# One PSUM bank for the values, two for the first layer, and all orders made anew, in a macaron block on one core

## The reference, cut to what matters

```
def kernel_func(q, k):
    scores = einsum('bhqd,bhkd->bhqk', q, k) / sqrt(8)
    w = relu(scores)
    return w / (sum(w, axis=-1, keepdims=True) + 1e-6)
def attn(x):
    qkv = (x @ w_qkv).reshape(B, S, 16, 24)          # q, k, v of 8 each
    out = einsum('bhqk,bhkd->bhqd', kernel_func(q, k), v)
    y = x + out.reshape(B, S, 128) @ w_out + b_out
    return layernorm(y) * gamma + beta
def ffn(x):                                          # w1: 128 x 512, w2: 512 x 128
    h = layernorm(x) * ln_gamma + ln_beta
    return x + 0.5 * (silu(h @ w1 + fc1_bias) @ w2 + fc2_bias)
x = x + 0.5 * ffn(layernorm(x))
x = x + attn(layernorm(x))
x = x + 0.5 * ffn(layernorm(x))
```

## Time and profile before

| | us |
|---|---|
| median of three runs | 380.73 (380.62 to 382.76) |
| the profiled execution | 380.02 |
| its span, first to last instruction | 378.2 |
| TensorE busy | 368.9 (98%) |
| VectorE busy | 286.9 (76%) |
| ScalarE busy | 227.5 (60%) |
| GpSimd busy | 222.8 (59%) |
| mean granted clock of TensorE | 0.995 of 2.4 GHz |

### The profile page before, as it was taken

One profiled execution on the slowest core, in us unless ns is written; L12 is line 12 of the kernel. 1 busy time (PEld: TensorE's weight loads), 2 busy tenths in 40 slices (PEclk: granted clock), 3 DMA queues, 4 the chain that ended last, 5 costly groups with the idle time before them and its releaser, 6 DMA issues.

```text
span 378.2 us, 11748 instructions
## 1 busy us (share of the span) xinstructions
PE 368.9 (98%) x4590; PEld 191.0 (51%) x4590; DVE 286.9 (76%) x690; ACT 227.5 (60%) x421; POOL 222.8 (59%) x454
## 2 busy tenths in 40 slices
PE   8979999999999999999999999999999999999996
PEld 7863523453554445553564445553464444523596
DVE  4744788987868978788777978789777877887681
ACT  2446466666857476566857577466766577466504
POOL 7683065737972589438981589437991567146053
PEclk9998999999999999999999999999999999999999
DMA  5156004600361005400271005410170004500001
GB/s 167 29 99 154 4 0 95 158 3 2 72 154 58 3 1 145 120 20 0 57 172 58 0 2 119 124 41 0 39 185 34 2 2 113 140 3 1 2 3 59
DMA packets 14391, 23.05 MB, mean 61 GB/s; under 512 B 2688, under 2 KB 3968, under 8 KB 14336
## 3 DMA queue, kind: packets, MB, share of 16 engines
q1 hardware_dynamic: 11520, 17.83, 19.5%
q10 hardware_dynamic: 2816, 4.46, 3.8%
HBM read 3.41 MB, written 2.10 MB: 15 GB/s over the span
## 4 chain that ended last, share of the span: by engine, by line
PE 89%; DVE 5%; issue 2%; POOL 2%; ACT 1%; DMA 1%; ACTq 0%; POOLq 0%; DVEq 0%
PE o_bank L461 31%; PE scores L446 16%; PE pre_bank L404 10%; PE post_bank L404 9%; PE pre_bank L409 5%; PE pre_bank L410 3%; PE post_bank L409 2%; PE pre_bank L397 2%; PE pre_bank L423 2%; PE post_bank L423 2%; PE post_bank L410 2%; PE o_bank L391 1%; DVE probs L990 1%; PE post_bank L397 1%; PE pre_bank L477 1%
## 5 line engine op out<-in xcount | busy, mean ns | idle before, releaser
L990 DVE TENSOR_SCALAR probs<-scores 128x512 f32<-128x512 f32 x256 | 164.0, 682 | 49.1 <-PE scores L446 46.9
L719 ACT ACTIVATE probs<-scores 128x512 f32<-128x512 f32 x256 | 138.6, 596 | 67.0 <-PE scores L446 67.0
L461 PE MATMUL o_bank<-probs,v_op 128*32 128x512 f32 x1024 | 136.4, 605 | 0.0
L446 PE MATMUL scores<-q_op,k_op 32*128 32x512 f32 x512 | 78.1, 494 | 2.0 <-DMA q_op<-q_parts 1.5
L446 PEld LDWEIGHTS scores<-q_op,k_op 32*128 32x128 f32 x512 | 32.0, 181 | 85.8 <-issue 50.7
L619 ACT ACTIVATE pre_y<-pre_bank,b_sum,col_consts 128x512 f32<-128x512 f32 x28 | 21.8, 779 | 26.4 <-PE pre_bank L423 26.3
L461 PEld LDWEIGHTS o_bank<-probs,v_op 128*32 128x32 f32 x1024 | 21.6, 108 | 30.3 <-issue 25.9
L404 PE MATMUL pre_bank<-w,pre_y 128*32 128x128 f32 x960 | 30.8, 274 | 0.0
L1019 POOL TENSOR_SCALAR norm_x_var<-norm_x_mv 128x4 f32<-128x4 f32 x21 | 4.1, 196 | 44.3 <-DVE norm_x_mv L791 43.8
L404 PEld LDWEIGHTS pre_bank<-w,pre_y 128*32 128x32 f32 x960 | 25.5, 110 | 7.9 <-issue 7.4
L404 PE MATMUL post_bank<-w,post_y 128*32 128x128 f32 x960 | 29.3, 273 | 0.0
(11 more groups left out here) (185 smaller groups left out, 548.6 us busy)
## 6 DMA issues: line engine op xcount, KB each, us to landing
k_op<-k_parts SPq DMA_DIRECT2D x64, 128.0 KB, 2.6
q_op<-q_parts SPq DMA_DIRECT2D x63, 128.0 KB, 2.7
pre_x<-in_L_attn_x_dram ACTq DMA_DIRECT2D x7, 256.0 KB, 2.7
out_dram<-o_rows ACTq DMA_DIRECT2D x7, 256.0 KB, 2.1
w_int<-in_L_ffn_fc_q_dram SPq DMA_DIRECT2D x2, 256.0 KB, 4.0
rows<-in_lines_dram ACTq DMA_DIRECT2D x1, 256.0 KB, 6.3
s_rows<-in_L_ffn_fc_scales_dram SPq DMA_DIRECT2D x1, 256.0 KB, 6.0
out_dram<-o_rows ACTq DMA_DIRECT2D x2, 128.0 KB, 2.3
```

Of the source, the lines that this page charges most:

```text
L446: mm(scores[i][:, j, :], k_op[rows, g, P * kt:P * (kt + 1)], q_op[rows, g, :], start=True, stop=True).then_inc(scores_done[i], 1)
L461: last = mm(o_bank[pair][VW * j:VW * (j + 1), :], v_op[:, kt, heads_of(g).start + 2 * j, :], probs[:, s % 2, j, :], start=(odd == 0 and kt ...
L719: activation(probs[:, s % 2, j, :], scores[0][:, j, :], ACT.Relu).then_inc(probs_done[0], 1)
L990: v.tensor_scalar(probs[:, s % 2, 2 + j, :], scores[1][:, j, :], 0.0, None, ALU.max).then_inc(probs_done[1], 1)
```

## The change

The second `o_bank` is given up and its bank given to `pre`, whose fills now take two banks in turn; the ten fills of a batch are an even number, so each kind of fill always has the same bank (`hT`, `fc1.1`, `fc1.3`, `uT`, `q` the first; `fc1.0`, `fc1.2`, `fc2`, `k`, `v` the second). Each bank has its own semaphore of reads, and a fill waits for the fill two before it. `fc1` waits for `hT` to be read ahead of its first product, since the bank no longer says so. The values of a new pair wait for the transpose of the pair before, where they waited for the one before that. All order tables are new. The number of matmuls does not change. The core of the diff, with one or two lines of the tables:

```diff
-    ([], ["post.fc2.0@-2", "pre.fc1.0@1"]),
-    (["post.fc2.1@-2", "post.fc2.2@-2", "post.fc2.3@-2", "pre.fc1.1@1"], []),
...
+    ([], ["post.fc2.0@-2"]),
+    (["post.fc2.1@-2"], ["post.fc2.2@-2", "post.fc2.3@-2", "pre.hT@1"]),
...
+            def place(self, b, fill):
+
+                i = len(self.fills) * b + self.fills.index(fill)
+                return i % len(self.banks), i // len(self.banks)
...
+            def freed(self, b, fill):
+
+                return self.free(b, fill), self.place(b, fill)[1] + 1
...
-        pre, post = Stage("pre", PRE_FILLS), Stage("post", POST_FILLS)
+        pre, post = Stage("pre", PRE_FILLS, 2), Stage("post", POST_FILLS, 1)
...
-        o_bank = [psum(f"o_bank{i}", [P, S]) for i in range(2)]
+        o_bank = psum("o_bank", [P, S])
...
-                if free_before(st, b, fill) > 0:
-                    pe.wait_ge(st.free, free_before(st, b, fill))
...
+                i, before = st.place(b, fill)
+                if before > 0:
+                    pe.wait_ge(st.frees[i], before)
...
                     next_fill(st, b, what)
+                    pe.wait_ge(*st.freed(b, "hT"))
...
-                    if not odd and NP * b + pair - 1 > 0:
-                        pe.wait_ge(o_read, NP * b + pair - 1)
+                    if not odd and NP * b + pair > 0:
+                        pe.wait_ge(o_read, NP * b + pair)
...
-                        last = by_tokens((pre.bank, o_bank[0])[h], aT, t, wo[:, :], True, True)
+                        last = by_tokens(pre.banks[h], aT, t, wo[:, :], True, True)
```

More of the change, by code:

```diff
@@ L131 @@
[L131 to L151 removed]
+    ["pre.u_apply@1"],
@@ L216, in __init__ @@
                 self.y = sb(f"{n}_y", [P, FT, S])
-                self.bank = psum(f"{n}_bank", [P, S])
-                self.full, self.free = sem(f"{n}_bank_full"), sem(f"{n}_bank_free")
+                self.banks = [psum(f"{n}_bank{i}", [P, S]) for i in range(banks)]
+                self.full, self.frees = sem(f"{n}_bank_full"), [sem(f"{n}_bank{i}_free") for i in range(banks)]
                 self.mixed = sem(f"{n}_mixed")
@@ L264, in half_bank @@
         def half_bank(st, h):
-            return ((pre, post) if st is pre else (post, pre))[h].bank
+            return ((pre, post) if st is pre else (post, pre))[h].banks[0]
         def of_half(first, whole, h, b):
@@ L363, in iteration @@
                     if g == 0:
-                        sp.wait_ge(pre.free, per * n + pre.n("k"))
+                        sp.wait_ge(*pre.freed(n, "k"))
                     for i in range(2):
@@ L427, in ffn @@
                         next_fill(st, b, "fc2")
-                    pe.wait_ge(st.free, len(st.fills) * b + st.n(f"fc1.{f}"))
+                    pe.wait_ge(*st.freed(b, f"fc1.{f}"))
                     for t in range(TT):
-                        last = by_tokens(st.bank, st.y[:, f, :], t, w2[:, f, :], f == 0 and t == 0, f == FT - 1 and t == TT - 1)
+                        last = by_tokens(st.bank(b, "fc2"), st.y[:, f, :], t, w2[:, f, :], f == 0 and t == 0, f == FT - 1 and t == TT - 1)
                     if f == FT - 1:
@@ L491, in task @@
                         if b > 0:
-                            pe.wait_ge(post.free, len(POST_FILLS) * b)
+                            pe.wait_ge(*post.freed(b - 1, "fc2"))
                         for t in range(TT):
-                            last = by_tokens(post.bank, aT, t, wo[:, :], True, True)
+                            last = by_tokens(post.banks[0], aT, t, wo[:, :], True, True)
                         last.then_inc(op_done, 1)
@@ L507, in edge @@
                     elif st is post and h == 0:
-                        pe.wait_ge(post.free, len(post.fills) * b)
+                        pe.wait_ge(*post.freed(b - 1, "fc2"))
                     elif st is post:
@@ L578, in work @@
                     if stage == "warm_up":
-                        warm_up(int(what))
+                        warm_up(int(what), pre.banks[1] if tb == 0 else o_bank)
                     elif what == "b1":
```

266 lines of the change are left out of this document (135 added, 131 removed).

## The result

The changed kernel takes 388.57 us (median of four runs, 388.46 to 388.68), the kernel before 381.03 beside it (380.62 to 382.76): a ratio of 1.019, with an interval of 1.016 to 1.023. It is slower by 7.5 us, and 0.8 above the forecast of 387.8. Its profiled execution has a span of 386.7, 8.5 more than before.

A forecast was written before the change was run, and what follows sets the result against it. Bound: TensorE's matmuls, and the evacuation of scores where matmuls leave it no cover. Steady batches 2.0, second 1.4, seventh 1.0, last 1.7 and end 1.7 sum to +7.8 on 380.02: 387.8 us, 8-in-10 range 382.5 to 391.

The forecast's parts named there:

- The steady batches: Third to sixth batch: waits +0.67, joins -0.17, so 43.5 us, +0.5 each and +2.0 together.
- step 8: Steady batch: x1 and its statistics ahead of ReLU(7) make the wait 0.94 instead of 0.52.
- step 10: Steady batch: fc1.0 follows its own transposes after one step; wait of 0 to 0.5, taken as 0.25.
- The end: Behind the last values: all 96 fc2 records after op push the last layer's transposes 1.65 later; +1.7.
- The second and the seventh batch: Second: bare steps at its seam and late values(0), +1.4; seventh: transposes now at step 1 and 0.5 more, +1.0.
- bare step: Step with nothing beside scores and values: values start 2.40 behind scores at the earliest, TensorE arrives at 1.88; costs 0.52.
- One values bank: I take 0: Values of steps 8 and 0 wait for the previous pair's transpose, but covered; 0, with 0.3 as high end.
- The prologue and the first batch: Prologue trades places, bound by the same q rows: 0, from -0.5 to +0.5; first batch gains and loses: 0.
- The last batch: x2, its statistics and a wait for GpSimd put ReLU(6) some 2.5 us behind its scores; +1.7, 0 to +2.5.
- rival 3: Clock drops after the new wait at the end and in thinner first steps, up to 1.9 each: 391; chance 0.15.
- Rival 1: Only sure terms: steady joins and waits cancel; end, transposes and part of last batch remain, +3, 383; chance 0.19.
- Rival 2: Steps 8 to 11: taking x1's statistics ahead frees the waits, if x1 starts within 1.3 of scores(6); 376.3; chance 0.08.

The follow-up runs named there:

- the filler: Changed kernel with 6 warm-up matmuls behind the values in step 3 of the last batch, ahead of scores(4); 390.79 us, ratio 1.026.
- the two of the same prologue named above: Changed kernel with k to v spread over steps 11 to 14 (387.48 us), and changed kernel with x1's statistics moved from step 6 to 7 (391.89 us).

## Why the prediction was right, and where it was not

**The steady batches: right.** +0.49 each against +0.5, with scores(8) and scores(14) standing still as forecast: 1.07 for the 0.94 of the sum, 0.53 for 0.52. The two errors in it are small and opposite: step 8 was 0.13 too low (x1 and its statistics take 1.93 on VectorE, 215.80 to 217.73, and not 1.80), step 10 (0.05 measured) 0.21 too high. Filling steps 13 and 14 gives 0.47 back; moving the statistics shows that they are half of the wait at scores(8).

**The end: right** in size (+1.72 for +1.7) and in cause, shown by putting two entries back.

**The second and the seventh batch: right in size,** within 0.13, but the second with some luck. At its seam scores(0) wait 0.53 and values(0) 0.52, near to what was forecast for each, and step 8 and the bare step at scores(14) cost what they do in a steady batch. Against this stands a gain that the forecast did not have: the wait of fc1.1 for ScalarE in the kernel before, 0.50 in this batch, is gone with the second bank. And the wait of values(0) ended with the transpose out of the single bank, 0.16 behind the v that I had named. The wait in the kernel before, then the one of values(0) in the changed kernel:

```profile
68.23 0.50 PE L409 MATMUL pre_bank<-pre_t_hi,w_hi 128*128 128x512 f32 x1 [0.43 <-ACT pre_y L619]
```

```profile
69.46 1.06 PE L480 MATMUL o_bank<-probs,v_op 128*32 128x512 f32 x8 [0.45 <-DVE o_t L828]
```

**"One values bank: I take 0" held for the steady batches of the changed kernel, and failed as a statement on the bank.** Values(8) do not wait there. But with the old orders the new banks cost 0.69 per batch, above the 0.3 that I had as the high end. I had looked for a wait of values(8), and put the transpose "right behind ReLU(8)" as free. The runs show that its place on VectorE costs this much with either number of banks. In the changed kernel the new order answers just this: x1's statistics are gone from step 8, where the transpose now stands (which makes scores(8) wait), and the four transposes of step 9 stand ahead of values(8) and cover their wait for the bank. So +0.5 was right, but I had booked it all on the order, where part of the order pays for the bank:

| x1's statistics | first `oT` | steps 13, 14 | steady |
|---|---|---|---|
| step 8 | step 12 | filled | 42.96 |
| step 8 | step 8 | filled | 43.65 |
| step 7 | step 8 | bare | 44.03 |
| step 6 | step 8 | bare | 43.46 |
| step 6 | step 8 | filled | 42.99 |

The last line is the answer to the change: with one values bank and the best of these orders the steady batch is as long as before. Its waits are 1.12 for 1.05, its matmuls 41.87 for 41.91; the orders give back 0.66 of the 0.69 that the new banks cost with the old ones.

**The prologue and the first batch: missed,** 0 for +1.09 and 0 for +0.48. "Bound by the same q rows" was true of the wait, but the rows are made from q, and q itself is later in the new order. The last product of q, in the changed kernel and in the one before:

```profile
22.49 0.28 PE L572 MATMUL scores<-pre_t_lo,wqk_hi 128*128 128x256 f32 x1
```

```profile
21.34 0.28 PE L553 MATMUL scores<-pre_t_lo,wqk_hi 128*128 128x256 f32 x1
```

The first scores start 5.68 and 5.74 behind it; with the old prologue the product is at 21.81 and the scores 5.72 behind. In all fourteen kernels this distance is 5.67 to 5.80, so q sets the start. I should have followed it through the new order instead of calling it a trade. How much of the 1.09 is the order's and how much the scatter of the start is an estimate only (0.7, above), and the 0.7 of the clock's early fall more than covers the 0.48: with the first scores at full clock the first batch of these orders took 37.64, where before it took 37.89.

**The last batch: +1.05 for +1.7, and for another reason.** The waits for the evacuation are not longer than before but shorter (4.4 us in all for 5.0: scores(4) 1.94, scores(7) 1.26, 1.2 in three more places). What was added are 1.44 us by matmuls at half clock: rival 3, at a place that I had not named. As the filler showed, these hide in part under the chain that leads to x2, so they can't simply be subtracted.

**The rivals.** Rival 1 (only the sure terms, 383) fell with the steady batches. Rival 2 fell at its own point: x1 starts at 215.80, 2.45 behind scores(6) and not within 1.3, and scores(8) stand still all the longer. Yet a part of it was true. The 0.35 of scores(10) in the kernel before is not bareness: scores, values and four transposes there give 0.44 + 1.00 + 0.59 + 0.44 = 2.47 of cover, more than the 2.40. ReLU(9) was late, at 174.03 and 1.07 behind its scores instead of 0.64, since x1's statistics stood ahead of it (172.84):

```profile
172.96 0.51 PE L446 MATMUL scores<-q_op,k_op 32*128 32x512 f32 x4
```

With the statistics gone from step 8, 0.05 is left of the waits at steps 10 and 11; the same statistics then cost scores(8) 0.54. This is read from the two traces, no run moves the statistics alone in the kernel before. Rival 3 had named two places. At the end of the kernel the clock stayed at 0.99; at the first steps the half clock lasted from 28 to 35 (0.52), where it had been some 3 us; and it came in the last batch, which the rival had not named.

## What to carry to other kernels

Where another engine's ReLU or copy paces TensorE, count the cover only between one issue into a bank and the next issue into it; work that stands behind the waiting instruction hides nothing. When a buffer is given up, price not the wait for it but the place that its early release forces on the engine that reads it. And when something in front of fixed filler grows, the filler must shrink by as much.

## What the runs showed of the hardware

TensorE's clock fell from 2.4 to 1.2 GHz in the middle of the kernel, behind an idle time of 0.86 (ahead of the rest of scores(4) in the last batch). The changed kernel at the start, behind the idle 2.62, and in the last batch (columns as above):

```profile
28.00:35.00 7.00, 6.18 (x28) 2.62 (x32) 2.87 (x5) 2.90 (x6) 6.57 (x15) 0.52 0.90 204
338.00:342.00 4.00, 4.00 (x28) 0.95 (x24) 2.77 (x6) 2.48 (x7) 1.45 (x2) 0.57 0.20 70
```

The busy share does not show it: TensorE counts as busy in all of 338 to 342. Of the kernels with the new orders on the new banks every one had such a stretch in its last batch (the changed kernel and seven variants of it); before and four variants of it had none, nor had the new orders on the old banks. Idleness alone did not decide: 1.74 us ahead of op at the end left the clock at 1.00, with 96 records and the warm-ups behind them. Nor did it at the start: behind idle times of 2.62 to 2.74 the clock was down before the first scores in the changed kernel and three of its variants, while in the two of the same prologue named above (2.66 and 2.72) it stayed at 1.00 until after 30. The Trainium skill ("TensorE: Matmul & The Clock Gate", The HAM clock gate) has activity as what releases the throttle; the rows agree in that the dense stretch behind op kept the full clock and the sparse steps 4 to 7 did not. Two kernels with one prologue (before, and the one with only the transpose moved) had the lower clock for some 3 and some 6 us at the same first steps. What decides between them was not tried.
